# Attention and FFN on one core: the last two products with the high value parts as one, in the value jobs of half 1

## The reference

```
x = x + attention(layernorm(x))      # q, k, v per head; causal softmax(q k^T / sqrt(128)) v; output product, summed over heads
x = x + ffn(layernorm(x))            # layernorm with gamma and beta, ternary weight 256x256, bias
```

## Time and profile before

| | us |
|---|---|
| median of 3 runs | 810.5 (810.34 to 811.31) |
| the profiled execution's own time | 810.04 |
| its span, first to last instruction | 808.2 |
| PE busy | 799.1 (99%) |
| DVE busy | 674.2 (83%) |
| ACT busy | 557.7 (69%) |
| POOL busy | 550.8 (68%) |

### The profile page before, as it was taken

How to read it: one execution, slowest core, us unless ns; L and a number is a source line. 1 busy time by engine, 2 the same in 40 slices (tenths; PEclk the granted TensorE clock), 3 DMA queues, 4 the chain that set the end, 5 groups by cost and what they waited for, 6 DMA issues and landing times.

```text
span 808.2 us, 14644 instructions
## 1 busy us (share of the span) xinstructions
PE 799.1 (99%) x4844; PEld 722.8 (89%) x4844; DVE 674.2 (83%) x1471; ACT 557.7 (69%) x1031; POOL 550.8 (68%) x282
## 2 busy tenths in 40 slices
PE   8999999999999999999999999999999999999997
PEld 7898999898899898899999899999899989899896
DVE  8987887887888888788888788788878788888998
ACT  6976766667676667766677777667676666677674
POOL 6278865696676956778557776568666685577585
PEclk9999999999999999999999999999999999999999
DMA  6466666555666556666555666655666655566503
GB/s 190 97 146 150 155 161 141 123 130 140 168 143 147 124 137 151 147 145 151 139 138 125 157 154 160 143 118 130 145 168 143 139 132 118 137 147 141 131 1 105
DMA packets 57242, 111.49 MB, mean 138 GB/s; under 512 B 16976, under 2 KB 21200, under 8 KB 57168
## 3 DMA queue, kind: packets, MB, share of 16 engines
q1 hardware_dynamic: 57168, 110.56, 57.1%
HBM read 10.88 MB, written 2.10 MB: 16 GB/s over the span
## 4 chain that ended last, share of the span: by engine, by line
PE 95%; DVE 2%; DMA 1%; ACT 1%; issue 0%; SPq 0%; DVEq 0%
PE scores L731 24%; PE ring L684 24%; PE ring L664 22%; PE ring L694 11%; PE ring L673 11%; PE ring L653 1%; PE scores L721 1%; PE ring L628 1%; DMA acc<-in_x 1%; DVE acc L981 0%; DVE turn L896 0%; DVE stats L926 0%; DVE xT L961 0%; ACT turn L822 0%; DVE scores L888 0%
## 5 line engine op out<-in xcount | busy, mean ns | idle before, releaser
L550 POOL TENSOR_TENSOR pT<-pT 128x1024 fp32r<-128x1024 f32 x186 | 447.2, 2408 | 224.6 <-ACT pT L829 221.8
L829 ACT ACTIVATE pT<-pT 128x1024 fp32r<-128x1024 f32 x186 | 197.4, 1062 | 173.9 <-DMA pT<-turn 173.8
L888 DVE CUSTOM_DVE_ANT_0 scores<-scores,mask 128x128 f32<-128x128 f32 (+7 forms) x256 | 194.7, 762 | 71.3 <-PE scores L731 69.6
L731 PE MATMUL scores<-kT,qT 128*128 128x512 f32 (+2 forms) x1056 | 228.9, 350 | 0.0
L896 DVE STREAM_TRANSPOSE turn<-turn 128x128 f32<-128x128 f32 (+1 forms) x248 | 184.8, 764 | 50.3 <-ACT turn L822 49.8
L822 ACT ACTIVATE turn<-scores,negmax 128x128 f32<-128x128 f32 (+7 forms) x256 | 188.0, 735 | 47.4 <-DVE negmax L888 46.4
L684 PEld LDWEIGHTS ring<-pT,v 128*128 128x128 f32 x1116 | 189.8, 189 | 26.4
L684 PE MATMUL ring<-pT,v 128*128 128x512 f32 x1116 | 209.4, 341 | 0.0
L731 PEld LDWEIGHTS scores<-kT,qT 128*128 128x128 f32 x1056 | 173.9, 189 | 17.5
L694 PE MATMUL ring<-wo_s,zT 128*128 128x256 f32 x768 | 112.8, 283 | 0.5 <-DVE zT L959 0.5
L908 DVE SCALAR_TENSOR_TENSOR acc<-ring,inv,acc 128x256 f32<-128x256 f32 x256 | 108.9, 467 | 0.1
(11 more groups left out here) (86 smaller groups left out, 549.4 us busy)
## 6 DMA issues: line engine op xcount, KB each, us to landing
pT<-turn SPq DMA_DIRECT2D x496, 128.0 KB, 2.3
pT<-turn SPq DMA_DIRECT2D x496, 64.0 KB, 2.0
acc<-in_x SPq DMA_DIRECT2D x8, 256.0 KB, 5.1
wk_raw<-in_wk SPq DMA_DIRECT2D x8, 256.0 KB, 3.4
wq_raw<-in_wq SPq DMA_DIRECT2D x8, 256.0 KB, 2.9
wv_raw<-in_wv SPq DMA_DIRECT2D x8, 256.0 KB, 3.0
norm<-in_wo SPq DMA_DIRECT2D x8, 256.0 KB, 3.1
out<-acc SPq DMA_DIRECT2D x7, 256.0 KB, 2.2
```

Of the source, the lines that this page charges most:

```text
L550: pool.tensor_tensor(chunk(half, LO, c), f32(chunk(half, LO, c)), f32(chunk(half, HI, c)), ALU.subtract).then_inc(plo_ready, 1)
L731: mm = pe.matmul(scores[:, t % 2, first + c:first + c + n], qT[:, par, a, t * P:(t + 1) * P], kT[:, par, m, c:c + n], start=(i == 0), stop ...
L829: act.activation(chunk(half, HI, c), f32(chunk(half, LO, c)), ACT.Copy).then_inc(phi_ready, 1)
L888: dve.tensor_tensor_reduce(out=tile, in0=tile, in1=mask[:, S - (t + 1) * P:S], scale=-1.0, scalar=FAR, op0=ALU.add, op1=ALU.min, accum_out ...
```

## The change

In the value jobs of half 1 (31 of them, units 0 to 30) the last key tile, of 128 columns, no longer takes three matmuls with 128 columns each. Its two products whose stationary operand is the high part of v become one matmul with 256 columns (both parts of the probabilities side by side) into `edge`, the last 256 columns of the even half of `scores`. The product with the low part of v still adds into the ring. On DVE a new item `edge` sums the two groups of 128 columns of `edge` into an SBUF tile `rest` and adds `rest` to the job's bank in the ring. ACT waits for that before it copies the job. PE waits before the edge matmul until the last even score tile's `exp` is over and the edge before was read, and before score tiles 4 and 6 until the edge is read. Value jobs of half 0 and of the last unit stay as they were.

The tables of all engines are new, those of the start and the end too. `("ff", 7)` is one job now, with one add and one store. `ident_b` now lies in `rest`, and `stats` has four places instead of sixteen.

```diff
+    edge_no, edges_issued, tile_there, there = {}, {}, {}, None
+    for item in tensor_run:
+        if item[0] == "pv" and item[1] == 1:
+            tile_there[item] = there
+            edge_no[item[1:]] = len(edge_no)
+        elif item[0] == "s" and item[1] in (4, 6):
+            there = item[2] * QT + item[1]
+            edges_issued[item[1:]] = len(edge_no)
...
+        edge = scores[:, 0, 2 * BANK - 2 * P:2 * BANK]
...
-                for j in range(n_keys):
-                    for i in range(3):
-                        lo, (a, m) = unseen(half, j), PASSES[i]
...
+                edged = (half, u) in edge_no
+                for j in range(n_keys - 1 if edged else n_keys):
+                    for i, (a, m) in enumerate(PASSES):
...
+                j, lo = n_keys - 1, HALF - 1
+                if tile_there["pv", half, u] is not None:
+                    pe.wait_ge(probs_ready, tile_there["pv", half, u] + 1)
+                if edge_no[half, u] > 0:
+                    pe.wait_ge(edge_read, edge_no[half, u])
+                pe.matmul(edge.rearrange("p (m a i) -> p m a i", m=2, a=A), v[:, batch(u), HI, j, hh * E:(hh + 1) * E],
+                          pT[half][:, :, :, j, lo * Q:P], start=True, stop=True)
+                return pe.matmul(blocks[:, :, lo * Q:P], v[:, batch(u), LO, j, hh * E:(hh + 1) * E],
+                                 pT[half][:, HI, :, j, lo * Q:P], start=False, stop=True)
...
+                if edges_issued.get((t, u), 0) > 0:
+                    pe.wait_ge(edge_read, edges_issued[t, u])
...
-                    act.wait_ge(job_done, job[item] + 1)
+                    if kind == "pv" and item[1:] in edge_no:
+                        act.wait_ge(edge_added, edge_no[item[1:]] + 1)
+                    else:
+                        act.wait_ge(job_done, job[item] + 1)
...
+            def add_edge(half, u):
+
+                item = ("pv", half, u)
+                dve.wait_ge(job_done, job[item] + 1)
+                dve.tensor_reduce(rest[:, :], edge.rearrange("p (m c) -> p c m", m=2), AX_X, ALU.add).then_inc(edge_read, 1)
+                dve.wait_ge(edge_read, edge_no[half, u] + 1)
+                tile = ring_bank(item).rearrange("p (a c) -> p a c", a=A)[:, :, (HALF - 1) * Q:P]
+                dve.tensor_tensor(tile, tile, rest.rearrange("p (a i) -> p a i", a=A), ALU.add).then_inc(edge_added, 1)
```

More of the change, by code:

```diff
@@ L39 @@
 TENSOR = (
[3 rows of a table removed]
[3 rows of a table added]
 )
 SCALAR = (
[L45 to L48, removed]
+    ("exp", 0, 0), ("pv", 1, -2), ("exp", 1, 0), ("v", 1, -1), ("exp", 2, 0), ("hip", 1, 0, -1), ("qk", 1, 1),
@@ L54 @@
-    ("v", 1, 0), ("flip", 5, 0), ("max", 6, 0), ("max", 7, 0), ("qk", 3, 1), ("flip", 6, 0), ("flip", 7, 0),
-    ("qk", 1, 1),
+    ("max", 0, 0), ("v", 0, -1), ("edge", 1, -2), ("max", 1, 0), ("max", 2, 0), ("flip", 0, 0), ("pv", 1, -2),
+    ("v", 1, -1), ("flip", 1, 0), ("o", 0, -2), ("qk", 1, 1), ("o", 1, -2), ("max", 3, 0), ("flip", 2, 0),
+    ("max", 4, 0), ("inv", -1), ("flip", 3, 0), ("qk", 0, 1), ("pv", 0, -1), ("qk", 2, 1), ("max", 5, 0),
+    ("max", 6, 0), ("o", 2, -2), ("flip", 4, 0), ("max", 7, 0), ("flip", 5, 0), ("flip", 6, 0), ("flip", 7, 0),
@@ L56 @@
+    ("qk", 3, 1), ("o", 3, -2),
 )
 GPSIMD = (
-    ("split", "q", 1), ("lop", 0, 1, 0), ("split", "v", 0), ("lop", 1, 0, 0), ("lop", 1, 1, 0), ("lop", 1, 2, 0),
-    ("lop", 1, 3, 0), ("split", "k", 2), ("split", "o", -1), ("lop", 0, 0, 1),
+    ("lop", 0, 0, -1), ("lop", 0, 1, -1), ("split", "v", -1), ("lop", 1, 0, -1), ("lop", 1, 1, -1), ("lop", 1, 2, -1),
+    ("lop", 1, 3, -1), ("split", "k", 1), ("split", "o", -2), ("split", "q", 1),
 )
 SYNC = (
-    ("wave", 1, 1, -1), ("wave", 1, 2, -1), ("wave", 1, 3, -1), ("wave", 0, 0, 0), ("wave", 0, 1, 0), ("load", -1),
@@ L63 @@
-    ("wave", 0, 2, 0), ("wave", 0, 3, 0), ("wave", 1, 0, 0),
+    ("wave", 1, 0, -1), ("wave", 1, 1, -1), ("wave", 1, 2, -1), ("wave", 1, 3, -1), ("wave", 0, 0, 0),
+    ("wave", 0, 1, 0), ("wave", 0, 2, 0), ("load", -4), ("wave", 0, 3, 0),
 )
@@ L93 @@
[L93 to L97, removed]
+    ("x", 1), ("stat", 4), ("stat", 5), ("stat", 6), ("qk", 2, 0), ("x", 2), ("x", 3), ("qk", 0, 0), ("stat", 7),
@@ L103 @@
-    ("lop", 0, 0, 2),
+    ("split", "k", -1), ("split", "q", -1), ("clear", 1), ("split", "v", -1), ("lop", 0, 0, 0), ("lop", 0, 1, 0),
+    ("lop", 1, 0, 0), ("lop", 1, 1, 0), ("lop", 1, 2, 0), ("lop", 1, 3, 0), ("split", "o", -1),
 )
@@ L201, in exists @@
             return u % KINDS == (2 if item[1] == "v" else 3) and u < LAST - 1
-        if kind in ("flip", "wave", "hip", "lop", "pv"):
+        if kind in ("flip", "wave", "hip", "lop", "pv", "edge"):
             return 0 <= u < LAST
@@ L230, in last_of @@
         return max(job[kind, a, u] for a in parts) + 1
+    edge_no, edges_issued, tile_there, there = {}, {}, {}, None
[6 more added lines that the diff above has]
+            edges_issued[item[1:]] = len(edge_no)
+    assert list(edge_no) == [i[1:] for i in vector_run if i[0] == "edge"]
     low_order = [i for i in gpsimd_run if i[0] == "lop"]
@@ L311, in attention_ffn @@
         ident = sb("ident", [P, P], F32)
-        ident_b = sb("ident_b", [P, P], BF16)
+        rest = sb("rest", [P, P], F32)
         mask = sb("mask", [P, S], BF16)
@@ L331, in attention_ffn @@
         shift = std
+        ident_b = rest[:, 0:P // 2].bitcast(BF16)
+        edge = scores[:, 0, 2 * BANK - 2 * P:2 * BANK]
         x_in = [sem(f"x_in{g}") for g in range(NT // 2)]
@@ L680, in weighted_v @@
                 pe.wait_ge(plo_ready, chunk_no[half, CHUNKS[half] - 1, u] + 1)
-                for j in range(n_keys):
-                    for i in range(3):
-                        lo, (a, m) = unseen(half, j), PASSES[i]
-                        mm = pe.matmul(dst.rearrange("p (a c) -> p a c", a=A)[:, :, lo * Q:P],
-                                       v[:, batch(u), a, j, hh * E:(hh + 1) * E], pT[half][:, m, :, j, lo * Q:P],
-                                       start=(j == 0 and i == 0), stop=(j == n_keys - 1 and i == 2))
-                return mm
+                blocks = dst.rearrange("p (a c) -> p a c", a=A)
+                edged = (half, u) in edge_no
+                for j in range(n_keys - 1 if edged else n_keys):
+                    for i, (a, m) in enumerate(PASSES):
+                        lo = unseen(half, j)
+                        mm = pe.matmul(blocks[:, :, lo * Q:P], v[:, batch(u), a, j, hh * E:(hh + 1) * E],
+                                       pT[half][:, m, :, j, lo * Q:P], start=(j == 0 and i == 0),
+                                       stop=(j == n_keys - 1 and i == 2))
+                if not edged:
+                    return mm
+                j, lo = n_keys - 1, HALF - 1
[7 more added lines that the diff above has]
+                                 pT[half][:, HI, :, j, lo * Q:P], start=False, stop=True)
             def project_o(c, u, dst):
@@ L925, in statistics @@
                 for t in tiles:
[L926 removed]
+                    last = dve.bn_stats(stats[:, t % 4, :], acc[:, t, :])
                 last.then_inc(ln_step, 1)
@@ L929, in statistics @@
                 for t in tiles:
-                    last = dve.bn_aggr(mv[:, t, :], stats[:, t, :])
+                    last = dve.bn_aggr(mv[:, t, :], stats[:, t % 4, :])
                 last.then_inc(ln_step, 1)
@@ L988, in _ @@
                     flip_tile(*item[1:])
+                elif kind == "edge":
+                    add_edge(*item[1:])
                 elif kind == "inv":
```

50 lines of the change are left out of this document (25 added, 25 removed), and 57 rows, old and new, of tables (END_SCALAR, END_TENSOR, END_VECTOR, START_TENSOR).

## The result

The changed kernel takes **812.28 us** (811.49 to 813.75, 12 runs) against 810.23 us before (809.79 to 811.95, 12 runs) on the same chip. The ratio is 1.0026, 95% interval 1.0018 to 1.0034: slower by 0.26%. The forecast was 806.9 us, faster, in a range of 805.0 to 810.2. Sign and range are both wrong. The experiments ran beside the kernel before on other chips, where its median was 810.29 to 810.35 us; ratios are to those runs.

What follows compares the result with a forecast made beforehand. PE's issue distances, plus ramp and tail, were taken to bound the kernel. 810.04 - 3.4 (edge) - 0.2 (start and end) = 806.4 us for the profiled execution, 806.9 us against the median; range 805.0 to 810.2.

Steps and rivals of the forecast that it cites:

- What bounds the kernel: Whole kernel: time is the sum of PE's issue distances, plus a ramp at the start and a tail.
- The edge matmul, -3.4 us: Half-1 value jobs: three load slots become two, 0.11 us less in each of 31 jobs.
- A: Rival at the edge: the old trio really costs 0.28 us, gain only 1.6 us, time 808.7; chance 0.10.
- D: Rival at the edge: matmuls not paced by loads, nothing changes, 810.3 us, or a 0.4 us gain; chance 0.03.
- The waits on PE, 0: PE around the edge matmul: exp and edge read finish in time, so no cost.
- DVE's new item, 0.7 us: DVE's sum and add per edge: 0.43 + 0.28 us, 22 us over 31 units, none of it PE's.
- The deadline: DVE's take of the value job, behind the edge: done at 5.0 us against PE asking at 5.37; price 0.
- B: Rival at the ring: DVE's take over 0.4 us later than counted, PE stops every unit; 815.6 us at 0.3 over; chance 0.07.
- PE's work per unit is otherwise the same ... Price 0.: Steady unit, the other moved jobs: they cost PE nothing.
- Start, 0: Start of the kernel: jobs of equal length swapped, 0, with 1 us either way.
- End, -0.2 us: End of the kernel: better cover -0.5, last add and store +0.3; ends' sum between -1.6 and +1.5 us.
- Rival C: Ramp and tail: the new tables lose 2 us or more at the ends, 808.9 us; chance 0.10.

Runs made afterwards that it cites:

- m1: Separate kernel of only weight loads and matmuls of given widths on PE, computation left out; a trio turned into a pair gives 0.101 us.
- e1: Kernel before with the edge alone added, in the old orders: 808.63 us, ratio to before 0.9978.
- e2: Changed kernel without the edge, three matmuls of 128 columns again, new orders kept: 815.56 us, ratio to before 1.0063.
- e7: e1 with the value job of unit 30 left as it was before, so without the last edge: 807.82 us, ratio to before 0.9967.
- e8: e7 with the edge also in half 0's value jobs, units 1 to 29, and a v job between score tiles 4 and 5: 810.53 us, ratio 1.0000.
- e5: Changed kernel with DVE's inverse of unit 31 put behind the ready output job at the end: 811.90 us, ratio to before 1.0018.
- e6: e5 with job ff 1 also put ahead of the last output job on PE and DVE: 812.82 us, ratio to before 1.0032.
- e3: Changed kernel with the v job ahead of score tile 7 on PE, tile 5's flip before tile 7's minimum on DVE: 811.44 us, ratio to before 1.0016.

## Why the prediction was wrong

*What bounds the kernel.* Right: the middle is the sum of PE's issue distances.

*The edge matmul, -3.4 us.* Right, with 0.10 us each instead of 0.11. m1 gives 0.101 us for the trio turned into a pair, the kernel 0.095 in e1's middle; e2 to after is -3.3 us in all. The moving operand in eight runs costs next to nothing: 124 ns from the edge matmul to the next start, where others of 256 columns have 120. Weight loads of the changed kernel, start us, us:

```profile
418.77 0.19 PEld L709 LDWEIGHTS scores<-pT,v 128*128 128x128 f32 x1
418.89 0.19 PEld L711 LDWEIGHTS ring<-pT,v 128*128 128x128 f32 x1
```

They stand 0.12 apart, and the next, for score tile 0, comes at 419.01: as forecast within 0.01. Rivals A and D are out. The distances of the old trio are 0.28 us, as A had it, but the matmul behind it has some 0.05 more, so it does cost three load slots. In D, the 0.4 us set the page's 0.243 for the trio against 0.23 for the pair, which was read from the trace.

*The waits on PE, 0, and DVE's new item, 0.7 us.* Right. PE never waits for the edge. The item has 415 and 299 ns in the groups by line, 0.71 us, or 22.2 over 31 units. DVE as a whole is busy only 16.6 us more: its instructions' durations add up to 20.7 more, and they overlap, which busy time counts once. In the queue the two parts take 0.45 and 0.21:

```profile
420.79 0.41 DVE L932 TENSOR_REDUCE rest<-scores 128x128 f32<-128x256 f32 x1
421.24 0.30 DVE L935 TENSOR_TENSOR ring<-ring,rest 128x128 f32<-128x128 f32 x1
...
423.30 0.65 DVE L998 TENSOR_TENSOR zT<-ring,zT 128x512 fp32r<-128x512 f32 x1
```

*The deadline.* Right, 5.0 against 5.37 foreseen. The timeline has L748 at 419.07 and the take's end at 423.95, so 4.88; the `o` job asks at 424.47, so 5.40. The wait for tile 2's scores was 0.67 and not 0.5. B didn't come. (One reading in it was wrong, without effect: three flips follow tile 7, not four.)

*"PE's work per unit is otherwise the same ... Price 0."* **This is the step that failed.** I priced a moved job by its own matmuls, and said that the moves cost PE nothing. The matmuls are the same, but their sum depends on what stands beside them. The kernel before begins four long stretches of 512 columns per unit behind narrower ones: tile 3 with both `qk` jobs and the value job of half 0; tile 5; two `qk` jobs with tile 6; tile 7 with the value job of half 1. The changed one begins six: one `qk` with tile 3; one with the value job of half 0; one with tile 5; one with tile 6; tile 7; the value job of half 1. The records give 2.53 us of excess before and 4.85 after, 2.3 us in the middle, or 0.08 per unit, of which shorter distances of narrow matmuls behind them give back 0.01. The count alone doesn't make it up. In ns, the four before lose 24, 8, 27 and 27, the six after 41, 8, 36, 28, 27 and 27: two more at 27 are 0.05 us of the 0.08, and the rest lies in the 41 behind tile 2 (384 columns; in m1 too the longer distances go on further behind 384) and the 36 behind the narrow end of a value job. Over 29 units the orders so cost 2.1 us in undisturbed units. Stalls of single units add 1.0 us, in units 2, 5 and 7, with the 0.3 of ACT's `exp` above among them; before they are 0.2. That is 2.9 us, as much as the edge saves there. The rows to see it stood in the trace of before: the chain has `qk` pairs at 2.73 and 2.75 us, and the x6 stretch of 512 columns behind the narrow `o` job at 1.39, where six at the pace inside a stretch would be 1.36.

*Start, 0.* Wrong by 1.1 us. The new orders start worse in every kernel that has them (55.17 to 56.61, against 54.42 to 55.01 in before, e1, e7 and e8, whose starts are the old one). But the same tables spread over 1.4 us from one execution to the next, so the size is uncertain. In after a wait of PE for xT of 0.9 us is part of it (the last section tells it); in e5 that wait is 0.2, and the start is as long, 55.59, with 1.3 us of waits for ACT's norms and 0.6 for an `exp`. Which part the orders cause by themselves stays open.

*End, -0.2 us.* Wrong by 1.1 us, and by 0.3 in the tail. I had counted the gain of one `ff` job more behind the last transposes, and not where DVE takes things: the inverse ahead of a ready `o` job, and the last zT behind more work. How much each of these costs isn't shown, since e5 and e6 won back at most 0.24 us. That two more edges load DVE was named and not priced; one of them costs 0.57 us in the old orders (e1 to e7). The last add takes 0.69 us, as forecast.

Rival C, ramp and tail worse by 2 us or more, had its size right (2.3 us over before) and a chance of 0.10. It was thought of alone. With the middle's gain in place C gives 809; it took C and the lost middle together to get to 812.3, and no rival said that the middle's gain could be eaten by the orders.

Sum, against the profiled before: -3.1 for 31 edges, and over that +1.2 in the start, +2.1 for the orders and +0.8 for stalls in the middle, +1.0 in the end, and +0.3 of tail: with rounding +2.2 us, the difference of the spans.

## What to carry to other kernels

When jobs are moved, price the neighbourhoods too: here a stretch of 512-column matmuls loses mostly 0.02 to 0.03 us each time it begins behind narrower ones (0.01 to 0.04 in the units of this kernel), so keep wide jobs together, and look at the beginnings per unit before and after, and at what stands in front of each. Split a change that brings a saving with new orders into its two halves on the chip: the saving was worth 2.4 us by itself, with the last edge left out, and the new orders cost 5.3. At the end of such a pipeline try leaving new work out of the last unit: here that was worth 0.57 us (e1 to e7).

## What the hardware showed that was not expected

**The slow beginning.** It is told above: 233, 236, 228, 233, 231 ns and then 227, behind 448 columns or fewer, not behind 496. Its price is mostly 0.02 to 0.03 us, which no single row shows; what the new orders added of it is 2.3 us, 0.3% of this kernel. The Trainium skill, TensorE: Matmul & The Clock Gate, section Back-to-back issue gap, gives N over 2.4 plus 2.5 ns for an isolated matmul, 216 ns for 512 columns, and 131 ns sustained. The runs here agree with neither: they have 227 within a stretch, a load with each, and up to 236 at its beginning, so that the gap depends on the neighbour too.

**A tiny DVE instruction that waits for POOL.** At the start of the changed kernel a DVE instruction of 4 elements per partition takes 1.15 us; in the kernel before the same one takes 0.16. DVE and POOL of the changed kernel (start us, us), then DVE before:

```profile
9.48 1.15 DVE L979 SCALAR_TENSOR_TENSOR std<-mv,rstd 128x4 f32<-128x4 f32 x1
10.55 0.68 DVE L998 TENSOR_TENSOR xT<-ring,xT 128x512 fp32r<-128x512 f32 x1
```

```profile
9.34 1.27 POOL L558 TENSOR_TENSOR wq_s<-wq_raw,wq_s 128x512 fp32r<-128x512 f32 x1
```

```profile
9.47 0.16 DVE L940 SCALAR_TENSOR_TENSOR std<-mv,rstd 128x4 f32<-128x4 f32 x1
```

It started 0.14 us after POOL's instruction and ended with it (10.63 and 10.61). In the kernel before it began in the last 0.13 us of a POOL instruction, which ended at 9.60, and was through at 9.63. Behind it DVE's xT is late and PE waits 0.9 us, against 0.4 and 0.2 in e3 and e5, which have the same start and took 0.16 us for the small instruction. It is a matter of chance in part: POOL's place depends on when the weights land, and among nine profiled kernels three (after, e2, e6) have it at this place. The Trainium skill, SBUF — State Buffer, section Who interferes with whom, says that a DVE instruction with two SBUF inputs contends with a GpSimd instruction that reads SBUF, that the shared ports are an exclusive lock, and that issue order decides who blocks. By that the small one, issued second, waits until POOL's is done, and these rows agree.
